# Weight sums between the pieces of another step, x turned in a new order, gate inverses a step earlier

## The reference, cut to what matters

```python
xn = layernorm(x)
q, k, v = xn @ Wq.T, xn @ Wk.T, xn @ Wv.T        # 32, 8 and 8 heads of 128
q, k = rmsnorm(q) * q_norm_w, rmsnorm(k) * k_norm_w
scores = q @ k.T / sqrt(128) + slope[head] * (key - query)   # causal
s = concat_heads(softmax(scores) @ v) @ Wo.T
h = xn @ lora_A.T ;  lora = h @ (lora_B * 2 * lora_weights)
g = silu(xn @ W.T + bias + lora)
x + s * g
```

## Time and profile before

| | us |
|---|---|
| median of 3 runs | 2909.21 |
| lowest, highest | 2906.86, 2913.39 |
| the profiled execution | 2908.81 |
| its span | 2906.9 |
| PE busy | 2658.3 (91%) |
| DVE, ACT, POOL busy | 1741.1, 1771.0, 1684.1 (60%, 61%, 58%) |
| L913, low parts of weights on POOL | 986.9, 448 times |
| mean granted clock of TensorE | 0.963 |

### The profile page before, as it was taken

One profiled execution on the slowest core, in us unless ns is written; L12 is line 12 of the kernel. 1 busy time (PEld: TensorE's weight loads), 2 busy tenths in 40 slices (PEclk: granted clock), 3 DMA queues, 4 the chain that ended last, 5 costly groups with the idle time before them and its releaser, 6 DMA issues.

```text
span 2906.9 us, 39948 instructions
## 1 busy us (share of the span) xinstructions
PE 2658.3 (91%) x13840; PEld 2341.4 (81%) x13840; DVE 1741.1 (60%) x3544; ACT 1771.0 (61%) x4627; POOL 1684.1 (58%) x821
## 2 busy tenths in 40 slices
PE   3668888888989999999989999999999999999997
PEld 2557777777878888888878888888877888888886
DVE  4445665556555666556656675655566575555566
ACT  2255555545666666666666666667666666766663
POOL 3366556656655576665555666566555665655643
PEclk8879999999999999999999999999999999999999
DMA  7767556665634433333423443333422543333323
GB/s 246 248 213 236 209 185 228 230 210 177 237 110 137 143 124 109 118 115 114 144 86 114 144 129 110 120 114 105 144 89 86 179 131 115 106 112 115 110 83 120
DMA packets 184119, 424.48 MB, mean 146 GB/s; under 512 B 34544, under 2 KB 75632, under 8 KB 183024
## 3 DMA queue, kind: packets, MB, share of 16 engines
q1 hardware_dynamic: 183920, 421.93, 44.4%
HBM read 349.51 MB, written 89.13 MB: 151 GB/s over the span
## 4 chain that ended last, share of the span: by engine, by line
PE 74%; DVE 8%; DMA 5%; ACT 5%; POOL 4%; SPq 3%; issue 3%; POOLq 0%; DVEq 0%; ACTq 0%
PE proj L477 18%; PE proj L479 17%; PE proj L478 17%; PE tr L570 4%; PE sc L477 3%; DMA wu<-xtok 3%; PE sc L478 2%; PE sc L479 2%; PE ot L478 2%; PE ot L479 2%; PE tr L550 2%; PE ot L477 2%; POOL wl L913 2%; SPq L295 1%; DVE pT_lo L1093 1%
## 5 line engine op out<-in xcount | busy, mean ns | idle before, releaser
L913 POOL TENSOR_TENSOR wl<-wl,wh 128x896 fp32r<-128x896 f32 x448 | 986.9, 2232 | 720.6 <-ACT wh L696 720.4
L477 PE MATMUL proj<-wh,xh 128*128 128x448 f32 x1792 | 679.9, 379 | 84.3 <-POOL wl L913 59.7
L478 PE MATMUL proj<-wl,xh 128*128 128x448 f32 x1792 | 665.6, 371 | 0.0
L479 PE MATMUL proj<-wh,xl 128*128 128x448 f32 x1792 | 665.2, 371 | 0.0
L924 POOL TENSOR_TENSOR wb_lo<-wb_lo,wb_hi 128x1024 fp32r<-128x1024 f32 x128 | 307.8, 2404 | 414.2 <-ACT wb_hi L706 414.2
L763 ACT ACTIVATE prob<-prob,negmax 128x128 f32<-128x128 f32 (+3 forms) x512 | 286.6, 564 | 339.9 <-DVE negmax L1128 339.9
L1150 DVE TENSOR_TENSOR acc<-acc,proj 128x512 f32<-128x512 f32 x480 | 327.5, 683 | 216.1 <-PE proj L479 214.4
L696 ACT ACTIVATE wh<-wl 128x896 fp32r<-128x896 f32 x448 | 406.8, 964 | 79.3 <-DMA wl<-wu 79.1
L477 PEld LDWEIGHTS proj<-wh,xh 128*128 128x128 f32 x1792 | 342.6, 191 | 123.6 <-issue 67.7
L477 PE MATMUL proj<-o_hi,wb_hi 128*128 128x512 f32 x1024 | 428.4, 418 | 12.3 <-issue 6.1
L479 PE MATMUL proj<-o_hi,wb_lo 128*128 128x512 f32 x1024 | 407.2, 398 | 0.0
(11 more groups left out here) (121 smaller groups left out, 4498.0 us busy)
## 6 DMA issues: line engine op xcount, KB each, us to landing
wl<-wu SPq DMA_DIRECT2D x448, 448.0 KB, 3.9
wb_lo<-wo_in SPq DMA_DIRECT2D x128, 512.0 KB, 3.3
wu<-xtok SPq DMA_DIRECT2D x98, 448.0 KB, 4.4
wo_in<-wo SPq DMA_DIRECT2D x32, 512.0 KB, 5.5
xtok<-wa SPq DMA_DIRECT2D x56, 256.0 KB, 4.1
gate_dram<-z_buf SPq DMA_DIRECT2D x32, 256.0 KB, 5.1
xtok<-wa SPq DMA_DIRECT2D x56, 128.0 KB, 4.1
xtok<-xT SPq DMA_DIRECT2D x28, 256.0 KB, 5.2
```

The lines of the kernel that those rows point to most:

```text
L477: pe.matmul(out, hi_l, hi_r, start=first, stop=False, skip_group_check=onto)
L478: pe.matmul(out, hi_l, lo_r, start=False, stop=False, skip_group_check=onto)
L479: return pe.matmul(out, lo_l, hi_r, start=False, stop=last, skip_group_check=onto)
L913: pool.tensor_tensor(w_slot(wl, w), w_slot(wl, w, True), w_slot(wh, w), ALU.subtract).then_inc(w_ready, 1)
```

## The change: what it does

- SP: in j = 0 the loads of half 0 of `new` go ahead of P6 and P7; in j = 1 the stores of half 0's raw tiles go ahead of P4; in j = 2 the stores of half 0's sums, the wait for them and the loads of half 1 go ahead of P3. `store_result(ending, 0)` moves from (0,2) to (0,1), ahead of P5. x of batches 2 and 3 is loaded in (3,3) instead of (5,3).
- VectorE: all four weight sums of half 0 between the pieces of (g,1). The gate quarters are inverted in (g,0) after the pieces (in head 7 before a new batch between the pieces of (7,1)), the multiplication always in (g,1). Turned x gets its low part one piece later than before.
- The statistics of x are taken in (5,1) for batches 2 and 3 (`ln_group`), as before in (6,1) for batch 1. ScalarE scales all four parts in (6,1) for batches 2 and 3; for batch 1 two in (6,2) and two in (6,3) between pieces.
- x: the order of products is P1, P2, P7, P4, P6, P5, P3 (before P4, P1, P2, P6, P7, P5, P3), with four tiles in (6,3), six in (7,0), four in (7,1). The sums of x are at the head of GpSimd's steps: P7 and P6 in (7,0), P5 and P3 in (7,1). `finish` and `weight_sums` go ahead of both products' low parts.

```diff
-FILLS = [P4, P1, P2, P6, P7, P5, P3]
+FILLS = [P1, P2, P7, P4, P6, P5, P3]
-    at = {(6, 3): range(0, 4), (7, 0): range(4, 8), (7, 1): range(8, 12), (7, 2): range(12, 14)}
+    at = {(6, 3): range(0, 4), (7, 0): range(4, 10), (7, 1): range(10, 14)}
+def ln_group(b):
+    return 6 if b == 1 else 5
...
                 if j == 0:                                    # SP
                     store_sums(n + 1, 1)
-                    load_product(n + 1, P6)
-                    load_product(n + 1, P7)
                     if new is not None:
                         sp.wait_ge(prep_tst[1], 64 * new)
                         load_weights(new, 0)
                         load_gate_weights(new, 0)
+                    load_product(n + 1, P6)
+                    load_product(n + 1, P7)
                 if j == 1:
-                    load_product(n + 1, P4)
                     if new is not None:
                         store_halves(new, 0)
+                    load_product(n + 1, P4)
+                    if g == 0 and ending is not None:
+                        store_result(ending, 0)
                     load_product(n + 1, P5)
                 if j == 2:
-                    load_product(n + 1, P3)
                     if new is not None:
                         store_sums(new, 0)
                         sp.wait_ge(prep_tst[0], 64 * (new + 1))
                         load_weights(new, 1)
                         load_gate_weights(new, 1)
+                    load_product(n + 1, P3)
...
-                if (g, j) == (6, 2) and b + 1 < BATCH:        # ScalarE
-                    ln_scale(b + 1, 2)
-                    ln_scale(b + 1, 3)
+                if (g, j) == (6, 1) and 0 < b < BATCH - 1:
+                    for t in range(NT):
+                        ln_scale(b + 1, t)
+                if (g, j) == (6, 2) and b == 0:
+                    ln_scale(1, 0)
+                    ln_scale(1, 1)
...
                 bias_of(m + 1)                                # GpSimd
+                    if (g, j) == (7, 0):
+                        x_sum(next_x, P7)
+                    if (g, j) == (7, 1):
+                        x_sum(next_x, P5)
                 low_b(v + 1)
+                    if (g, j) == (7, 0):
+                        x_sum(next_x, P6)
+                    if (g, j) == (7, 1):
+                        x_sum(next_x, P3)
                 if j == 3 and n + 2 < HKV:
-                    weight_sums(n + 2)
-                low_product(*[(n + 1, P6), (n + 1, P4), (n + 1, P3), (n + 2, P1)][j])
+                    weight_sums(n + 2, 1)
                 if g == 0 and b > 0 and j in (1, 3):
                     finish(b - 1, j // 2)
+                low_product(*[(n + 1, P6), (n + 1, P4), (n + 1, P3), (n + 2, P1)][j])
...
                 for i, u in enumerate(pieces):                # VectorE
+                    if turned:
+                        x_lo(turned.pop(0))
                     if fills:
-                        x_lo(fills.pop(0))
+                        turned.append(fills.pop(0))
+                    if (j, p, t) == (0, P2, 0):
+                        gate_sum(n)
+                    if j == 1 and n + 2 < HKV:
+                        weight_sum(n + 2, 0, (P5, P7, P6, P4)[i])
+                    if j == 1 and late_gate:
                         gate_inverse(n, i)
+                if j == 0 and not late_gate:
+                    for quarter in range(4):
+                        gate_inverse(n, quarter)
-                if n + 2 < HKV:
-                    if j == 1:
-                        weight_sum(n + 2, 0, P5)
-                        weight_sum(n + 2, 0, P7)
-                    if j == 2:
-                        weight_sum(n + 2, 0, P6)
-                        weight_sum(n + 2, 0, P4)
```

More of the change, by code:

```diff
@@ L453, in step @@
                     store_gate(n)
[L454 removed]
+                    if g == 3 and 0 < b < BATCH - 1:
                         load_x(b + 1)
@@ L666, in step @@
                     out_ready(v)
-                    out_proj(v, 0)
-                    out_proj(v, 1)
+                    for c in range(2):
+                        out_proj(v, c)
+                        if fills:
+                            turn_x(fills.pop(0))
                 pe.wait_ge(prob_ready, m + 1)
@@ L952, in x_sum @@
+                    pool.tensor_tensor(r11, r21, r11, ALU.add).then_inc(sum_ready, 1)
+                if what == P3:
                     pool.wait_ge(tr_done, TR["x", b, 3] + 1)
[L953 to L959, removed]
-                c = 4 * g
[L961 to L967, removed]
+                    pool.tensor_tensor(r12, r12, r21, ALU.subtract).then_inc(sum_ready, 1)
@@ new lines, in weight_sums @@
+            def weight_sums(g, h):
+                b11, b12, b21, b22 = (prep_tile(g, h, a, c) for a in range(2) for c in range(2))
+                c = 4 * g
+                pool.wait_ge(prep_bst[h], 48 * (g + 1))
+                pool.tensor_tensor(b11, b12, b11, ALU.subtract).then_inc(prep_t[h], 1)
+                pool.tensor_tensor(b12, b22, b12, ALU.subtract).then_inc(prep_t[h], 1)
+                pool.wait_ge(prep_t[h], c + 1)
+                pool.tensor_tensor(b22, b22, b11, ALU.subtract).then_inc(prep_t[h], 1)
+                pool.wait_ge(prep_t[h], c + 3)
+                pool.tensor_tensor(b21, b21, b22, ALU.subtract).then_inc(prep_t[h], 1)
@@ L1266, in step @@
                     scale_rows("q3")
-                    gate_sum(n)
-                if j == 2 and g == 6 and next_x:
+                if j == 2 and g == ln_group(b + 1) and next_x:
                     ln_factors(b + 1)
+                late_gate = g == 7 and next_x
+                pieces, fills = unit_pieces(n, j), x_fills(n, j)
+                turned = []
                 for i, u in enumerate(pieces):
@@ L1285, in step @@
                         scale_rows("q1")
-                if j == 1 and not more:
+                if j == 0 and not more:
+                    gate_sum(n)
+                if j == 0 and not late_gate:
                     for quarter in range(4):
                         gate_inverse(n, quarter)
-                late_gate = ending or (g == 6 and next_x)
+                turned += fills
+                if turned:
+                    x_lo(turned.pop(0))
                 add_out(v, 0)
+                if turned:
+                    x_lo(turned.pop(0))
                 if j == 2 and more:
                     row_factors(n + 1, 0)
-                if j == 2 and late_gate:
-                    gate_inverse(n, 0)
                 add_out(v, 1)
-                if j == 2 and late_gate:
-                    gate_inverse(n, 1)
+                if turned:
+                    x_lo(turned.pop(0))
                 for k in range(3):
@@ L1301, in step @@
                     scale_rows("k")
-                if j == 1 and not late_gate:
+                if j == 1:
                     gate_product(n)
```

53 lines of the change are left out of this document (17 added, 36 removed).

## The result

The changed kernel takes 2830.3 us (median of 3 runs, 2830.2 to 2835.9) against 2909.2 before: ratio 0.973, 95% interval 0.971 to 0.975. The forecast was 2823. Its profiled execution has a span of 2828.3 us, 78.6 less than before.

The account below looks back on a forecast made before the run. TensorE, 91% busy, was taken as the bound, with recoverable loss in the first six heads and the changes of batch. 2908.8 - 43 (first batch) - 42 (changes of batch) = 2823.8, stated as 2823 us; range 2764 to 2870.

Parts of the forecast that it names:

- (a): VectorE's weight sums between the pieces of (g,1), step j=1 of head g: four priced 6.4 to 12 us; 27.0 to 21.6 us.
- (b): Gate inverses in (g,0): four of 0.95 us fit VectorE's 4.83 us idle; undisturbed heads change by 0.
- (c): SP's new order makes P3 late in (g,2), plus 3.3 us (24.7), and P6 in (g,0), plus 1.0 (23.7).
- (d): In (g,3) the stand-stills for P1's late weights and late probabilities go: 21.4 us against 27.5, minus 6.1.
- (e): Steps about three changes of batch: shorter (6,2), (6,3), (7,2), (0,2), longer (7,0), (7,1); minus 41.6 us in all.
- (f): The start: sums of x move behind the gate rows' products, hidden by DMA; 0 us, between -1 and +3.
- A: Rival on the wait in (g,2): P3 is there in time, heads of 82 us, 2767 us; chance 0.18.
- B: Rival: both waits of (c) grow until the first batch gains nothing, heads of 98.6 us, 2866 us; chance 0.14.
- C: Rival: slower than before, the queue couples preparation to the running head; heads from 105.6 us, 2917 at 107; chance 0.05.
- D: Rival: waits on sums of x in (7,0) and (7,1) do not come, 3 x 11 less, 2790 us; no separate chance.

## Why the prediction was right

**(a) Right in size and place; a sum was priced too high.** (g,1) takes 21.4 us in the mean of heads 1 to 5 (21.6 said), with no gap before its scores. The first two of the four sums on VectorE, and GpSimd's two instructions of that time:

```profile
655.22 1.09 DVE L1188 TENSOR_TENSOR xtok<-xtok 128x896 f32<-128x896 f32 x1
...
657.25 2.66 DVE L1190 TENSOR_TENSOR xtok<-xtok 128x896 f32<-128x896 f32 x1
```

```profile
654.09 1.59 POOL L939 TENSOR_SCALAR bias_sb<-rel_sb,slope 128x512 f32<-128x512 f32 x1
656.57 2.39 POOL L931 TENSOR_TENSOR wb_lo<-wb_lo,wb_hi 128x1024 fp32r<-128x1024 f32 x1 [0.90 <-ACT wb_hi L711]
```

A sum that meets nothing takes 1.08 or 1.09 us, as the third and fourth do; the one beside GpSimd's 2.39 us takes 2.66. Both that the step ends had before, 1.63 and 2.95, were delayed. The four together take 5.9 us, less than the 6.4 to 12 of the sum. By the Trainium skill (SBUF — State Buffer, "SBUF: two separate sides") a VectorE instruction of two SBUF inputs and a reading GpSimd one exclude each other. For this pair the trace agrees: the sum takes 2.66 - 1.09 = 1.57 us more than alone, and GpSimd's instruction ran on for 1.71 us after it began. For GpSimd's bias instruction, which reads an SBUF tile too, the trace does not agree, as far as the rough ends of GpSimd's instructions tell: it ran until 655.68, the first sum began beside it at 655.22 and took 1.09 us all the same, and in head 0 the two ran side by side for 1.40 us and the sum took 1.47. So two of the four sums stood beside a GpSimd instruction, as said, but only one was held up; why the bias instruction holds none up, no run here shows.

**(b) Right.** The undisturbed heads keep 78.82 to 78.86 us; the inverses in (g,0) cost nothing. What they bring to (g,1) was not in the sum: 0.7 us a head by the run with the inverses in (g,1).

**(c) Right in place and kind, too small in size.** From the first issue of (g,2), at 668.29, P3 is issued after 17.0 us (16.2 said) and landed after 21.8 (20.5): 0.7 of it is the landing of the stores, 0.5 P3's own. TensorE stands 8.60 us (7.2), and 15.3 + 8.6 + 2.2 = 26.1 is what the trace shows, 26.2 in the mean of heads 1 to 5 (24.7 said). In (g,0) P6 needed 6.2 us from issue to landing, not 4.3, right behind 12 loads still in flight: ScalarE was late by 3.5 us (1.9), TensorE by 3.4 (1.6), and (g,0) takes 25.4 (23.7). Both together are 3.2 us a head of heads 1 to 5, 16 us; head 0, at 90.1 us, gives back 1.3 of its 91.4.

**(d) Right in size, the cause only in part.** (g,3) 21.3 us, 21.4 said. The sum named P1's late weights and late probabilities. The longest wait of ScalarE in this step before the change was another, for the step's output weights, issued at 732.07 behind the twelve loads:

```profile
736.50 1.06 ACT L706 ACTIVATE wb_hi<-wb_lo 128x1024 fp32r<-128x1024 f32 x1 [8.68 <-DMA wb_lo<-wo_in]
```

With the old order of the queue and the sums already between the pieces, (g,3) stays long (26.8 us in head 4): its gain comes from the order of SP.

**(e) Right step by step, too small in the sum.** Said and measured at the second change of batch: (6,2) 15.3, 15.3; (6,3) 23.0, 22.8; (7,0) 30.1, 30.1; (7,1) 28.6, 28.2; (7,2) 15.3, 15.3; (0,2) 15.5, 15.8. At the third change (7,0) and (7,1) take 31.5 and 29.1, with the granted clock at 0.89 and 0.88. TensorE's waits for the sums of x were 3.94 and 3.64 us (3.9 said). What the sum left out: (1,0) of the next batch, 22.6 us before, takes 21.2, three times 1.4; (6,0) at the first change, 21.2 for 22.8; (0,3), 2.3 in all three; and (6,3) fell by 1.3 more in all than said. On the other side stand the 2.3 us of heads 13 and 21.

**(f) Nearly right.** The start gives 1.3 us, just beyond the -1 to +3 of the sum.

So the first batch gave 13 us less than was expected and the changes of batch 8 more: 2823.8 + 13.0 - 7.8 + 2.3 - 1.3 = 2830.0. More than half of the one error took back the other, and that is luck: the total of 2830 against 2823 looks better than its terms.

**The rivals.** A was not this kernel, but its price was right: with P3 in time 2771.7 us was measured, 2767 said, and the first six heads took 83.5 us in the mean, 82 said. B and C did not come: heads 1 to 5 took 92.6 to 96.0 us, not 98.6 or more, and TensorE's only gaps over 0.5 us in them are the one in (g,0), 2.4 to 4.2 us, and the one in (g,2), 8.5 to 9.4, both ended by VectorE's maximum; GpSimd's sums of half 1 made none. D did not come either: GpSimd's first sum of x was ready 5.8 us after the marker of (7,0) (5.9 said). With the sums taken a step earlier it is worth 33 us, as it said.

## What to carry to other kernels

A queue that issues transfers in order and waits for a landing is an engine in its own right: put the loads that a running step needs between the stores and the wait for them, where the queue would only stand, and neither ahead of the stores, where P3 had to wait for its buffer and held them back, nor behind what follows the wait. When transfers are put in a new order, ask of each load that falls back who wants it and when: here the gap before the scores went from (g,1) to (g,2), and the new order of the queue gained nothing in the first six heads until P3 was moved. Before a wait is priced at its own length, ask which engine holds it in its order, and what stands behind: about half of what the late P3 cost reached TensorE only because ScalarE took a ready tile second.

## What the runs showed of the hardware

- Idle times of the same length cost different clocks. TensorE stood 3.38 us at 648.19 in the changed kernel, and the granted clock of the step stayed 1.00; in the run with P3 mended it stood 3.44 us at 596.99, and the step's clock was 0.87, which is 26.8 x 0.13 x 2 = 7.0 us at 1.2 GHz. In head 4, 2.91 us at 552.88 came with 0.93. With 3.94 us in (7,0) of the second change of batch it was 0.94 (3.6 us at 1.2 GHz); at the third change the same 3.94 us (2108.39) stood in a step of 31.5 us at 0.89 (6.9 us); with 8.60 us in (g,2) it was 0.80 (10.4 us).
- The twelve loads of a half cost SP 6.1 us of issuing (0.47 to 0.5 us each), as much as the stores ahead of them cost in flight beyond their issue. Four stores of 448 KB took 9.5 us from the first issue to the landing of the last, with nothing but two loads in front (669.61 to 679.16), and 9.5 again with P3 behind them (621.48 to 630.98).
